# Two self-attentions whose value products run in halves of 256 columns, one of them with its mask in VectorE's maximum

## The reference

```python
scores = jnp.einsum('bhqd,bhkd->bhqk', q, k) * scale
causal = jnp.triu(jnp.ones((S, S), dtype=bool), k=1)          # first layer only
scores = jnp.where(causal, jnp.finfo(scores.dtype).min, scores)
attn = jax.nn.softmax(scores, axis=-1)
out = jnp.einsum('bhqk,bhkd->bhqd', attn, v)
```

## Time and profile before

| | |
|---|---|
| Time, median of 3 runs | 4105.12 us (4092.93 to 4109.87) |
| The profiled execution | 4103.0 us, span of its trace 4101.3 us |
| Granted TensorE clock, whole span | 0.9 |
| Causal attention in the trace | about 156 to 760 us |
| Second self-attention in the trace | about 1540 to 2987 us |

### The profile page before, as it was taken

The page is one execution under the profiler, slowest core; times in us unless marked ns, Lnnn a source line. Parts: engine busy times, 40 slices in busy tenths (PEclk is TensorE's granted clock), DMA queues, the critical chain, the costliest instruction groups (busy, mean ns, idle before and its releaser), DMA issues. The chain is left out here.

```text
span 4101.3 us, 53675 instructions
## 1 busy us (share of the span) xinstructions
PE 3422.6 (83%) x19224; PEld 1734.9 (42%) x19224; DVE 2899.0 (71%) x4290; ACT 1964.8 (48%) x3821; POOL 833.8 (20%) x1135
## 2 busy tenths in 40 slices
PE   8499999767569868999999999999855769999758
PEld 5244444433358633333333333333343435554625
DVE  7567765345657779888888888888554457776375
ACT  3166665323223215777777777777721223334120
POOL 4222322123333340000000000000022434445000
PEclk9599988778779978999999999999977889999678
DMA  4311210000000240000000000000001231100202
GB/s 172 100 44 46 54 43 23 19 36 11 0 22 1 74 125 17 23 19 17 19 24 17 17 25 17 17 25 17 2 7 44 94 107 43 44 22 1 90 6 85
DMA packets 78651, 160.63 MB, mean 39 GB/s; under 512 B 21464, under 2 KB 38880, under 8 KB 78272
## 3 DMA queue, kind: packets, MB, share of 16 engines
q1 hardware_dynamic: 74176, 153.17, 12.5%
q10 hardware_dynamic: 4224, 4.19, 0.3%
HBM read 87.76 MB, written 54.72 MB: 35 GB/s over the span
## 5 line engine op out<-in xcount | busy, mean ns | idle before, releaser
L629 DVE TENSOR_REDUCE L_attn_tops<-L_attn_psM 128x2 f32<-128x1024 f32 (+3 forms) x1408 | 1561.3, 1148 | 315.1 <-PE L_attn_psM L739 311.5
L566 ACT ACTIVATE L_attn_E<-L_attn_psS 128x512 f32<-128x512 f32 (+3 forms) x2816 | 1388.2, 575 | 558.1 <-PE L_attn_psS L698 554.5
L698 PE MATMUL L_attn_psS<-L_attn_Q,L_attn_K 64*128 64x512 f32 (+3 forms) x2816 | 988.2, 434 | 125.2 <-ACT L_attn_E L566 100.7
L739 PE MATMUL L_attn_psM<-L_attn_K,L_attn_Q 62*128 62x512 f32 (+3 forms) x2816 | 1004.3, 478 | 56.3 <-DMA L_attn_K<-parts_k 30.7
L698 PEld LDWEIGHTS L_attn_psS<-L_attn_Q,L_attn_K 64*128 64x128 f32 x2816 | 468.2, 191 | 808.8 <-ACT L_attn_E L566 650.2
L714 PE MATMUL L_attn_psO<-L_attn_E,L_attn_V 128*32 128x512 f32 (+3 forms) x5632 | 727.2, 589 | 0.3 <-POOL L_attn_E L533 0.3
L739 PEld LDWEIGHTS L_attn_psM<-L_attn_K,L_attn_Q 62*128 62x128 f32 x2816 | 436.5, 193 | 150.7 <-issue 42.7
L524 POOL TENSOR_TENSOR L_AO<-L_attn_o 128x128 f32<-128x128 f32 x64 | 29.4, 459 | 1443.1 <-DVE L_attn_o L662 1443.1
L533 POOL TENSOR_SCALAR_AFFINE_SELECT L_attn_E<-L_attn_E 128x128 f32<-128x128 f32 x512 | 146.4, 292 | 455.8 <-ACT L_attn_E L566 443.9
L2193 ACT ACTIVATE x_E<-x_psS 128x512 f32<-128x512 f32 x256 | 138.9, 595 | 176.5 <-PE x_psS L2316 161.6
L2239 DVE TENSOR_REDUCE x_tops<-x_psM 128x2 f32<-128x1024 f32 x128 | 153.2, 1206 | 88.2 <-PE x_psM L2345 88.1
(11 more groups left out here) (346 smaller groups left out, 3838.2 us busy)
## 6 DMA issues: line engine op xcount, KB each, us to landing
parts_q<-L_proj_parts SPq DMA_DIRECT2D x64, 256.0 KB
parts_k<-L_proj_parts SPq DMA_DIRECT2D x64, 256.0 KB
L_attn_Q<-parts_q SPq DMA_DIRECT2D x192, 64.0 KB
L_attn_K<-parts_k SPq DMA_DIRECT2D x192, 64.0 KB
L_attn_Q<-parts_q SPq DMA_DIRECT2D x64, 128.0 KB
L_attn_K<-parts_k SPq DMA_DIRECT2D x64, 128.0 KB
queries<-x1p_qo SPq DMA_DIRECT2D x16, 512.0 KB
keys<-x1p_ko SPq DMA_DIRECT2D x16, 512.0 KB
```

What stands on the lines that cost most here:

```text
L566: act.activation(E[(4 * n + s) % 8][:, c0:], psS[bank][:, c0:], ACT.Exp, scale=scale).then_inc(e_done, 1)
L629: dve.tensor_reduce(dst, src, AX, ALU.max).then_inc(m_read, 1)
L698: pe.matmul(psS[bank][:, c0:], K[g.slot][r:r + RH, c, kt * P:(kt + 1) * P], Q[g.slot][r:r + RH, c, q * HALF + c0:(q + 1) * HALF], start=Tr ...
L739: last = pe.matmul(psM[bank][:, j * HALF:j * HALF + n], Q[t.slot][r:r + TOP, c, qt * P:(qt + 1) * P], K[t.slot][r:r + TOP, c, h * HALF:h * ...
```

## The change

Four things in `attend`:

1. The value product of a step is cut into two halves of up to 256 columns. The first half comes after the second slot of a step, the other after the fourth, where the whole product stood. In the causal attention a half that lies left of the diagonal is empty and is left out.
2. The causal attention computes the product of the step before last (BACK = 2) and has 12 tiles E in place of 8; the second attention keeps BACK = 1 and 8 tiles. `evacuate` and `turn_back` move with it.
3. `turn_maxima` now stands behind the last half product of step 0, where it stood ahead of the whole product.
4. The mask's matmuls are gone. For a masked pair VectorE now runs two `tensor_tensor_reduce` (one for each head): psM plus a tile `wide` (zeros, and the mask in its last 128 columns), written back to psM, with the maximum into tops. Unmasked pairs are reduced as before.

The diff, cut to its core:

```diff
+    BACK, HALVES = (2, 2) if causal else (1, 2)
+    RING = BACK + 1
-    BACK1, BACK0 = LATE + 2, LATE + ends[0] + 3
+    BACK1, BACK0 = LATE + BACK + 1, LATE + ends[0] + BACK + 3 - BACK
-        E = [m.sb(f"{tag}_attn_E{k}", [P, HALF]) for k in range(8)]
+        E = [m.sb(f"{tag}_attn_E{k}", [P, HALF]) for k in range(4 * RING)]
...
-                    act.wait_ge(o_done, g.times(NS, n + 1))
                     for s in range(4):
                         i, bank = s_item(t, place + s)
                         act.wait_ge(s_done, i + 1)
+                        if s == 0:
+
+                            act.wait_ge(o_done, g.times(NS, n + 1))
...
-                        if old and k == 0:
+                        if old and k == BACK - 1:
                             evacuate(t + -2, 1)
-                        if last and k == ends[0] + 1:
+                        if last and k == ends[0] + BACK:
                             evacuate(t + -1, 0)
...
+                    if masked:
+                        for j in range(2):
+                            row = (s + j) * TB + qt
+                            part = psM[bank][:, j * HALF:j * HALF + n]
+                            last = dve.tensor_tensor_reduce(part, part, wide[:, HALF - n:], 1.0, LOWEST,
+                                                            ALU.add, ALU.max, tops[:, row, h:h + 1])
+                        last.then_inc(m_read, 1)
+                        return
...
+                    lo, hi = max(c0, half * HALF // HALVES), (half + 1) * HALF // HALVES
+                    if lo >= hi:
+                        return
...
                     for s in range(4):
-                        last = pe.matmul(psO[32 * s:32 * s + 32, c0:HALF], V[g.slot][:, kt, s // shared, :],
-                                         E[(4 * n + s) % 8][:, c0:], start=(kt == 0), stop=(n == ends[q]),
+                        last = pe.matmul(psO[32 * s:32 * s + 32, lo:hi], V[g.slot][:, kt, s // shared, :],
+                                         E[(4 * n + s) % (4 * RING)][:, lo:hi], start=(kt == 0 and half == 0), stop=(n == ends[q]),
                                          skip_group_check=True)
-                    last.then_inc(o_done, 1)
+                    if half == HALVES - 1:
+                        last.then_inc(o_done, 1)
...
-                        if masked:
-                            for k in range(2):
-                                end = k * HALF + n
-                                pe.matmul(psM[bank][:, end - P:end], identb[:], maskb[:], start=True, stop=False, skip_group_check=True)
...
+                            if (s + 1) * HALVES % 4 == 0:
+                                products(t, n, last, old, (s + 1) * HALVES // 4 - 1)
                         if last and n == 0:
                             turn_maxima(t, 4 if old else 0)
-                        if live and step >= 1:
-                            product(g, step - 1, s_item(t, place)[0] + 3)
```

More of the change, by code:

```diff
@@ L354, in attend @@
     LATE = 5
+    BACK, HALVES = (2, 2) if causal else (1, 2)
+    RING = BACK + 1
+    assert NS * 4 % (4 * RING) == 0 and BACK < LATE
     assert NP2 == 2 * NS
@@ L423, in in_turn @@
             return range(NS if new or last else LATE + 5)
+        scored, count = {}, 0
+        for g in range(1, groups + 2):
+            for n in in_turn(g < groups, g <= groups):
+                at = (g - 1, n - LATE) if n >= LATE else (g - 2, NS + n - LATE)
+                if 0 <= at[0] < groups:
+                    scored[at] = count
+                    count += 4
+                if n == 0 and g <= groups:
+                    count += 1
         def s_item(t, j):
@@ L602, in _ @@
                 dve.memset(tops[:], LOWEST).then_inc(m_neg, 1)
-                dve.wait_ge(maskin, 16)
-                dve.tensor_copy(maskb[:], mask[:, 0, :]).then_inc(masks, 1)
-                dve.wait_ge(masks, 1)
+                if causal:
+                    dve.memset(wide[:], 0.0).then_inc(masks, 1)
+                    dve.wait_ge(maskin, 16)
+                    dve.wait_ge(masks, 1)
+                    dve.tensor_copy(wide[:, HALF - P:], mask[:, 0, :]).then_inc(masks, 1)
+                    dve.wait_ge(masks, 2)
                 dve.sem_inc(blank, 1)
@@ L699, in score, with product, products @@
                               Q[g.slot][r:r + RH, c, q * HALF + c0:(q + 1) * HALF], start=True, stop=True).then_inc(s_done, 1)
[L701 removed]
+                def product(at, n, half):
+                    g = At(at, None, 3)
                     q, kt, c0 = steps[n]
[L703 to L712 removed]
+                    lo, hi = max(c0, half * HALF // HALVES), (half + 1) * HALF // HALVES
+                    if lo >= hi:
+                        return
+                    if lo == c0:
+                        if n == 0 or steps[n - 1][0] != q:
+                            pe.wait_ge(o_out, g.times(2, q))
+                        if n == 0:
+                            pe.wait_ge(v_in, g.times(1, 1))
+                        if diagonal[n]:
+                            pe.wait_ge(e_cut, cuts(g, n + 1))
+                        else:
+                            pe.wait_ge(e_done, scored[at, n] + 4 + 3)
                     for s in range(4):
[L714 to L715 removed]
+                        last = pe.matmul(psO[32 * s:32 * s + 32, lo:hi], V[g.slot][:, kt, s // shared, :],
+                                         E[(4 * n + s) % (4 * RING)][:, lo:hi], start=(kt == 0 and half == 0), stop=(n == ends[q]),
                                          skip_group_check=True)
[L717 removed]
+                    if half == HALVES - 1:
+                        last.then_inc(o_done, 1)
+                def products(t, n, last, old, half):
+                    j = n - LATE - BACK
+                    if j >= 0 and last:
+                        product(t.base - 1, j, half)
+                    if j < 0 and old:
+                        product(t.base - 2, NS + j, half)
                 def turn_back(t, g, q, k):
@@ L727, in most @@
                 def most(t, p, j, at):
-                    s, qt, h, n, masked = pairs[p]
+                    s, qt, h, n, _ = pairs[p]
                     i, bank = m_item(t, at[p])
@@ L733, in most @@
                             pe.wait_ge(m_read, i + -1)
-                        if masked:
-                            for k in range(2):
-                                end = k * HALF + n
-                                pe.matmul(psM[bank][:, end - P:end], identb[:], maskb[:], start=True, stop=False, skip_group_check=True)
                     c, r = head(s + j)
                     last = pe.matmul(psM[bank][:, j * HALF:j * HALF + n], Q[t.slot][r:r + TOP, c, qt * P:(qt + 1) * P],
-                                     K[t.slot][r:r + TOP, c, h * HALF:h * HALF + n], start=not masked, stop=True,
-                                     skip_group_check=True)
+                                     K[t.slot][r:r + TOP, c, h * HALF:h * HALF + n], start=True, stop=True)
                     if j == 0:
```

29 lines of the change are left out of this document (9 added, 20 removed).

## The result

The changed kernel takes **3968.5 us** (median of 4 runs, 3963.4 to 3970.0) against 4107.5 for the kernel before (median of 4): ratio 0.9664, 95% interval 0.9636 to 0.9692. That is 139 us less; I had forecast some 40 less. The direction was right, the size was not, and the result lies far outside the range.

A forecast was written before the change was run, and what follows sets the result against it. It took the second attention's step as bound by TensorE waiting for ScalarE's exponential, the causal attention's TensorE as nearly full. 4103.0 less 37 (second attention) less 3 (causal) gave 4063 us, range 4030 to 4118.

The forecast's parts named there:

- The step of 2.48 us: Second attention: a plain step falls from 2.67 to 2.48 us, with no score waiting for the exponential.
- rival 2: Second attention: the second visit to the products eats the gain, step 2.70 us, time 4115; chance 0.19.
- rival 3: Causal attention: VectorE becomes the bound, its masked maximum at two clocks per column, time 4223; chance 0.12.
- These five steps save nothing; the wait only grows: Second attention, `turn_maxima` to a group's first score: no gain; wait for the mparts DMAs grows from 0.34 to about 1.2 us.
- 2 x 0.45 lost: Second attention: two evacuations a group each delay the next first half product by 0.45 us, 0.9 us lost.
- The last group saves 16 x 0.19 = 3: Second attention, last group, scores and products alone: 16 steps each 0.19 us shorter, 3 us saved.
- Net 3 us: Causal attention: 0.3 us a group saved, 5 us over 16, less 2 for the first group: 3 us.
- eight further visits: Causal attention: 20 visits to the products a group instead of 12 cost TensorE 2.9 us in all.
- The first group: Causal attention: the first group, which has only maxima, becomes 2 us slower.
- rival 1: More gain: shorter mparts wait prevents causal low-clock spells, 20 to 30 us, plus smaller evacuation loss; time 4035; chance 0.13.

The follow-up runs named there:

- before_merged_dma: The kernel before, with four DMAs of two heads each in place of the eight that write the maxima into Q: 4062.6 us, ratio 0.989.
- l0_halves_only: The kernel before, with half products two steps back in the causal attention alone, mask still in TensorE, ScalarE's wait moved: 4112.6 us, ratio 0.999.
- before_extra_dma: The kernel before, with a ninth 4 KB DMA ahead of the eight for the maxima, in the second attention alone: 4106.9 us, ratio 1.000.
- l1_halves_only: The kernel before, with half products in the second attention alone, mask still in TensorE, ScalarE's wait moved: 4027.2 us, ratio 0.981.
- mask_only: The kernel before, with the mask moved from TensorE to VectorE and ScalarE's wait moved, products whole and one step behind: 4047.8 us, ratio 0.986.
- merged_whole_back2: The changed kernel, with four DMAs for the maxima and whole products two steps back in the causal attention: 3940.0 us, ratio 0.959 to before.
- after_wait_old: The changed kernel, with ScalarE's wait for buffer E again ahead of its wait for the first score: 3987.1 us, ratio 0.971 to before.
- after_merged_dma: The changed kernel, with four DMAs of two heads each in place of the eight for the maxima: 3933.0 us, ratio 0.958 to before.

## Why the prediction was wrong

**Right.** The step of 2.48 us and each of its parts; that the second visit does not eat the gain (rival 2 fell); that VectorE's masked maximum runs at full rate, 0.72 us for 512 columns (rival 3 fell); that the transposes and evacuations take some of it back. The Trainium skill, "Vector Engine (DVE) Microarchitecture Reference", Points that are easy to get wrong, names a halved rate for two sources in SBUF that are not bf16. Here one source is in PSUM, and the 0.72 us agree with reading the rule as not reaching that case.

**"These five steps save nothing; the wait only grows"** failed. I read one group's wait of 0.34 as the rule. It was one of four in 32. There SP's eight issues began at 2220.79 and the score stood at 2228.26, 7.47 us later; in a usual group of the changed kernel they began at 2207.07 and the score that waits for them stood at 2213.59, 6.52 us later:

```profile
2207.07 5.34 SPq L507 DMA_DIRECT2D L_attn_Q<-L_attn_mparts  x8
```

From `turn_maxima` to the first score a usual group took 11.88 us (1815.60 to 1827.48), and not the 12.29 of the earlier trace rows. With 0.44 of room before, four steps shorter by 0.19 bring 0.32 us of wait, and 0.35 was seen. Of 16 x 0.19 = 3.0 us, 2.7 arrive, not 2.1.

**"2 x 0.45 lost" at the evacuations** was 2 x 0.26: right mechanism, wrong size. So 2.7 less 0.5 is 2.2 a group; 1.99 was measured, and the last 0.2 lies around the transposes and `turn_maxima`, where I had 0.1.

**The moved wait** I quoted in the diff and priced at nothing, without a row. It was worth 0.05 us a step, and before the change that stood on the path, since the fourth score waits for the first exponential: 24 us in the second attention alone. In the changed kernel no score waits, so there it is worth 0.08 a group. Both edits remove the same wait; 44.40 to 43.63 by the one, to 42.45 by both.

**"The last group saves 16 x 0.19 = 3"** was 6.0 us: from its first score to its last transposes it takes 45.92 us before and 39.97 after. Without maxima products a step is 2.25 us, not 2.48, where before it was 2.67 either way.

The second attention so: 31 x (44.40 - 42.41) = 62 us, and the last group's 6 make the 68.

**"Net 3 us" in the causal attention** failed twice. At full clock a group gained 1.77 us, not 0.3: I priced VectorE's masked pair at 1.56 where it takes 1.26, and added a wait of TensorE for VectorE step by step that is mostly not there (5 us in all between 200 and 690). I priced the eight further visits at 2.9 us a group; beside the mask's matmuls they cost 2, without them 0.4. The gain is about 27 us over 15 periods. The first group, which I had 2 us slower, is no slower: its first score stands at 192.26 where it stood at 193.88 before.

The rest, 45 to 50 us, is the clock. As an estimate, the low clock costs 602 x 0.14 = 84 us before (from 156 to 758) and 529 x 0.06 = 32 after. By the windows above, some 11 us of the difference lie in the cold start, 25 in the middle and 13 in the tail (length times what the clock lacks to 1.00). My rival 1 named the spells in the middle, gave them 0.13 and 20 to 30 us, and tied them to a shorter wait for mparts; the wait grew. Nothing in the prediction has the other two. The cold start's low clock ends at 199 to 206 us in all eight kernels that have the mask in VectorE, and at 214 to 267 in the six that have it in TensorE; why is not shown.

**What the spells hang on.** In the trace of the kernel before, ten of the first scores that follow the cold start waited 0.98 us and no spell began there; four waited 1.39 to 2.28 us and a spell began at each (336, 537, 612, 688); two more fell into the tail behind the last group with maxima. In each of those four stretches an instruction fetch ran beside the eight DMAs, but so it did in some without. Two runs speak for the waits as the cause. In before_merged_dma no first score waits, and the spells between 220 and 668 us are gone. In l0_halves_only the DMAs are still eight, but its groups are longer, eleven of the fourteen first scores between 267 and 738 us do not wait, and there is no spell there. The loads of Q and K that follow each first score are not what does it alone: the same load runs at full clock in before_merged_dma.

```profile
327.00:335.00 8.00, 7.96 (x63) 3.77 (x62) 6.16 (x8) 5.46 (x14) 3.49 (x12) 1.00 0.70 183
```

But the length of the wait doesn't decide it. The causal attention of before_extra_dma is that of the kernel before, unedited, and there two of ten waits of 0.91 us were followed by a spell of 10 us (271 and 476); in l1_halves_only it was three of ten (266, 470, 576). Waits of 1.31 are followed by spells 8 times in 10 in mask_only, those of 1.30 once in 7 in the changed kernel, where one of 2.04 has none either; l0_halves_only has one of 1.61 without; and merged_whole_back2 has four short spells with no wait at all. What makes the difference no run isolates, so the cause of these 45 to 50 us stays open. So does where a spell falls: after_wait_old changes the period by 0.05 us and moves the time by 19 us through it.

## What to carry to other kernels

Before a wait in one row is used as a bound, count the periods that show it; how much room a chain has is measured by adding one small transfer to it. Price every line of a diff that touches an engine whose start another engine waits for, the order of two waits too. And where TensorE idles at one place per period for about a microsecond, look at the clock behind it: in before_merged_dma the groups became shorter by 15 us in all, and the time fell by 44.

## What the runs showed of the hardware

- ScalarE starts its exponential 0.54 us after the score's start if the wait for the score comes first and that for the long-free buffer second, and 0.59 the other way round. Why the order matters, no row says.
- VectorE's sum-with-maximum, PSUM in and out with a second source in SBUF, takes 0.31, 0.45, 0.58 and 0.72 us on average for 128, 256, 384 and 512 columns; its accumulator read is shown at 0.141 us and hidden under the next instruction.
- SP's issues of eight DMAs of 4 KB take 5.34 us from first to last in a usual group of the second attention (after), those of four of 8 KB 2.42 us (after_merged_dma): no more for one of twice the size.
- In the second attention a second visit to the products costs 0.15 us a step more than one (2 x 0.57 against 0.99), with nothing further at the scores around it.
